# Tail of the first graph layer with sigmoids and masks a step ahead, and the loops of the attention and message layers written out

## The reference

```python
# L0: gated sum over edges, then a GRU and a batch norm
att = sigmoid(x[src] @ W_att[:d] + x[dst] @ W_att[d:] + b_att)
aggregated = segment_sum((x[src] @ W_msg + b_msg) * att, dst)
# L1, three times: attention over the incoming edges
logits = sum(q[dst] * k[src], -1) / sqrt(d)
alpha = softmax of logits within each dst
agg = segment_sum(alpha[:, None] * v[src], dst)
# L3: an MLP of edge features gives weights, multiplied with x[src]
tpw = silu(silu(edge_feats @ A1 + b1) @ A2 + b2) @ A3
message = segment_sum(mji(tpw, x[src], edge_attrs), dst) / 10
```

## Time and profile before

| | |
|---|---|
| median of 3 runs | 7610.16 us (7602.88 to 7610.16) |
| the profiled execution | 7606.87 us, its span 7605.1 us |
| PE, DVE, ACT, POOL busy | 73%, 63%, 28%, 67% of the span |
| attention layers, first to last gather | 1607 to 2674, 2775 to 3832, 3934 to 4989 us |
| message layer, first to last gather | 6449 to 7537 us |
| tail of the first layer | about 1130 to 1463 us |

### The profile page before, as it was taken

The page is one execution under the profiler, slowest core; times in us unless marked ns, Lnnn a source line. Parts: engine busy times, 40 slices in busy tenths (PEclk is TensorE's granted clock), DMA queues, the critical chain, the costliest instruction groups (busy, mean ns, idle before and its releaser), DMA issues. The chain is left out here.

```text
span 7605.1 us, 137273 instructions
## 1 busy us (share of the span) xinstructions
PE 5586.2 (73%) x30113; PEld 4217.7 (55%) x30114; DVE 4809.0 (63%) x20423; ACT 2121.2 (28%) x5508; POOL 5100.1 (67%) x5173
## 2 busy tenths in 40 slices
PE   5664454667767777776777766769899897898887
PEld 4432223345656655666655556656566654676665
DVE  7974433555666655666754766674454545888887
ACT  1033332131111141111141111143343332555554
POOL 5788772447777747777747777737657474777774
PEclk6687777877888787888887888889999998989988
DMA  9422232146677746777746767756667574222222
GB/s 308 122 68 63 71 76 53 36 126 197 205 207 205 205 148 194 208 206 205 209 152 188 210 206 206 206 151 207 176 198 211 161 216 120 55 55 55 55 54 52
DMA packets 911521, 1149.47 MB, mean 151 GB/s; under 512 B 143137, under 2 KB 676193, under 8 KB 911009
## 3 DMA queue, kind: packets, MB, share of 16 engines
q1 hardware_dynamic: 689200, 673.54, 29.4%
q0 software_dynamic: 202464, 461.07, 22.6%
q10 hardware_dynamic: 19346, 9.66, 0.5%
HBM read 882.09 MB, written 261.74 MB: 150 GB/s over the span
## 5 line engine op out<-in xcount | busy, mean ns | idle before, releaser
L486 POOL DMA_INDIRECT G<-table_kv,idx x2496 | 2377.4, 952 | 959.1 <-issue 762.3
L1554 DVE SCALAR_TENSOR_TENSOR sums<-ramp,place,bank 128x128 f32<-128x128 f32 x2496 | 721.9, 343 | 1001.1 <-PE bank L1501 813.5
L1939 POOL DMA_INDIRECT G<-table_h,src_idx x864 | 824.6, 954 | 485.4 <-issue 256.3
L1473 ACT COPY slab<-bank 128x512 f32<-128x512 f32 x624 | 364.9, 585 | 2485.0 <-PE bank L1492 2480.4
L1492 PE MATMUL bank<-ident,G 128*128 128x128 f32 x2496 | 627.7, 338 | 570.9 <-DMA G<-table_kv,idx 565.2
L1501 PE MATMUL bank<-qT,slab 128*128 x4992 | 916.2, 341 | 166.1 <-issue 144.4
L486 POOL DMA_INDIRECT G<-table_h,idx x832 | 835.4, 1004 | 299.3 <-issue 231.3
L534 PE MATMUL bank<-OH,sums 128*128 128x128 f32 x4992 | 858.7, 327 | 143.4 <-DVE sums L523 122.1
L1501 PEld LDWEIGHTS bank<-qT,slab 128*128 128x128 f32 x4992 | 810.6, 246 | 258.4 <-issue 257.9
L514 DVE TENSOR_SCALAR OH<-ramp,place,weight 128x128 f32<-128x128 f32 x2262 | 805.2, 359 | 151.2 <-issue 81.2
L534 PEld LDWEIGHTS bank<-OH,sums 128*128 128x128 f32 x4992 | 763.7, 234 | 195.0 <-issue 73.0
(11 more groups left out here) (342 smaller groups left out, 8868.2 us busy)
## 6 DMA issues: line engine op xcount, KB each, us to landing
stash<-G SPq DMA_DIRECT2D x312, 512.0 KB
sums<-stash SPq DMA_DIRECT2D x624, 256.0 KB
sums<-adjacency SPq DMA_DIRECT2D x294, 522.5 KB
adjacency<-same SPq DMA_DIRECT2D x49, 1184.0 KB
same<-adjacency SPq DMA_DIRECT2D x90, 522.5 KB
G<-table_kv,idx POOLq DMA_INDIRECT x2496
sums<-adjacency SPq DMA_DIRECT2D x48, 408.0 KB
table_kv<-G SPq DMA_DIRECT2D x72, 256.0 KB, 3.1
```

The lines of the kernel that those rows point to most:

```text
L486: pool.indirect_dma_start(G[:, s, 0:width], None, tab, bass.IndirectOffsetOnAxis(ap=idx[:, s:s + 1], axis=0)).then_inc(c_gather[s].sem, 16)
L1473: act.copy(quad(KT, q).rearrange("p s d -> p (s d)"), bank[q % 2][:, :]).then_inc(c_kt.sem, 1)
L1554: ins = dve.scalar_tensor_tensor(scratch[:, s % QUAD, :], ramp[:], place[:, bass.ds(t * SLOTS + s, 1)], bank[2 + q % 2][:, (s % QUAD) * P: ...
L1939: pool.indirect_dma_start(G[:, s, 0:D], None, table[l], bass.IndirectOffsetOnAxis(ap=src_idx[:, DENSE + t:DENSE + t + 1], axis=0)).then_in ...
```

## The change

It has two parts. In the tail of the first layer, ACT's `gates` of a step's quad now stand behind the sigmoids of the next step's mask, and DVE issues the mask (or the placement) of step n + 1 before the adds of step n; `mask(TAIL)` is issued ahead of the loop, and the two first `gate_inputs` ahead of the second mask. SP's, POOL's and PE's lists in the tail stay as they are. In the attention and message layers, the loops over pieces and turns on PE, ACT, DVE (and SP in the message layer) become Python loops: their code is emitted once for each round, with constants in place of registers. POOL's `gather_loop` and SP's loops in the attention layers stay loops.

```diff
-        def turns(engine, body):
-            with engine.Fori(0, TURNS - 1) as i:
-                body(i, False)
-            body(TURNS - 1, True)
+        def turns(body):
+            for i in range(TURNS):
+                body(i, i == TURNS - 1)
...
                     if n == TAIL:
                         gates(FIRST_QUADS)
                         gates(FIRST_QUADS + 1)
-                    if n >= TAIL:
-                        for q in tail_quads(n - TAIL):
+                    if n > TAIL:
+                        for q in tail_quads(n - TAIL - 1):
                             if q + 2 < RUN_QUADS:
                                 gates(q + 2)
+                for q in tail_quads(ALL_STEPS - TAIL - 1):
+                    if q + 2 < RUN_QUADS:
+                        gates(q + 2)
                 act.wait_ge(adj_used.sem, adj_used.at(ALL_STEPS))
...
+                def mask_or_place(n):
+                    if n < ALL_STEPS:
+                        mask(n)
+                    elif n < ALL_STEPS + MASK_CHUNKS:
+                        place_extra(n - ALL_STEPS)
+
+
+                mask_or_place(TAIL)
                 for d in range(TAIL_STEPS):
                     n = TAIL + d
-                    if n < ALL_STEPS:
-                        mask(n)
-                    else:
-                        place_extra(n - ALL_STEPS)
+                    if d == 0:
+                        gate_inputs(FIRST_QUADS)
+                        gate_inputs(FIRST_QUADS + 1)
+                    mask_or_place(n + 1)
                     if n < ALL_STEPS and chunk_before(n) is not None:
                         add_chunk(chunk_before(n))
                     if n > ALL_STEPS:
                         add_chunk(MASK_CHUNKS + n - ALL_STEPS - 1)
                     if d == 0:
-                        gate_inputs(FIRST_QUADS)
-                        gate_inputs(FIRST_QUADS + 1)
                         onehots_and_adds(FIRST_QUADS, None)
...
-        def pieces(engine, body):
-            body(0)
-            body(1)
-            with engine.Fori(0, PIECES - 2) as i:
-                body(i + 2)
-            body(PIECES)
-            body(PIECES + 1)
+        def pieces(body):
+            for c in range(PIECES + 2):
+                body(c)
...
-                with dve.Fori(0, TURNS - 2) as i:
-                    turn(i + 1, False, False)
+                for i in range(1, TURNS - 1):
+                    turn(i, False, False)
```

More of the change, by code:

```diff
@@ L1484, in piece @@
                             act_late_onehots((t - LAG) * QUADS + q + 2)
-            pieces(act, piece)
+            pieces(piece)
         def pe_attention(skip_terms):
@@ L1543, in piece @@
                             pe_sums(t - LAG, q, quad_loaded, v_rows, (4, 5), LATE)
-            pieces(pe, piece)
+            pieces(piece)
         def dve_attention():
@@ L1694, in piece @@
                             take(to)
-            pieces(dve, piece)
+            pieces(piece)
         def act_add_relu(outT):
@@ L2323, in turn @@
                             features(h, (i * 2 + (h + 2)) * PAIR)
-                turns(sp, turn)
+                turns(turn)
             @block.scalar
@@ L2370, in turn @@
                         onehot(i, 5)
-                turns(act, turn)
+                turns(turn)
             @block.tensor
@@ L2426, in turn @@
                         product3(i, 5)
-                turns(pe, turn)
+                turns(turn)
             @block.vector
```

## The result

The changed kernel took **7424.2 us** (median of 4 runs, 7420.3 to 7430.5) beside 7607.6 us (7602.9 to 7610.2) for the kernel before: ratio 0.9763, 95% interval 0.9748 to 0.9777, some 180 us. The forecast was 7439 us. The profiled execution took 7430.5 us with a span of 7428.7.

What follows compares the result with a forecast made beforehand. POOL's gathers bound the attention and message layers, a ring of engines waiting on each other the first layer's tail. 7606.9 - 140 (tail) - 28 (attention) + 0 (message layer) = 7439 us, range 7404 to 7478.

Steps and rivals of the forecast that it cites:

- The sum: Whole kernel: profiled 7606.9 us, less 140 for the tail and 28 for attention, message layer 0, gives 7439 us.
- Long steps: First layer's tail, steps with 418 columns: 7.25 us each after the edit, against 13.65 before.
- the ring: First layer's tail: PE, DVE and ACT wait on each other in turn, 13.65 us; afterwards DVE, ACT, DVE, 7.25 us.
- Short steps: First layer's tail, steps with 272 columns: 6.8 us each after the edit, against 12.8 before.
- Placement steps: Tail's last nine steps, where DVE writes the placement: PE nearly alone, 5.2 us each against 10.1 before.
- The floor of 5.0 from POOL: Placement steps: at PE's faster clock (4.8 us), POOL's 5.0 us of gathers would be the floor.
- The turn of the extra rows: Tail: taken as unchanged at 10.5 us, with ACT's copies still waiting for the same gates and the same product.
- Attention: Three attention layers written out: 28 us gained, four fifths of POOL's 35.5 us lost through DVE's stops at each round.
- rival (a): Only the tail gains, since the softmax burst causes POOL's loss at the attention loop's borders: 7467 us, chance 0.10.
- Message layer: Message layer written out: 0 gained, since nobody holds POOL up; range -25 to +25 us.
- (b): Tail gains less: POOL and DVE block each other at every mask, 9.5 us a step, 7519 us, chance 0.06.
- (c): Slower than before: streaming written-out code stalls engines in attention and message layers, 7654 us, chance 0.03.

## Why the prediction was right, point by point

**The sum** held: 7439 forecast, 7424.2 measured, inside 7404 to 7478. Of the 183 us between the medians (168 forecast by them) the tail has 151 where 140 were forecast, and attention 17 where 28 were. That these two misses cancel is luck; the mechanisms of both were right. The message layer's 7 is not the change's, as the run with that layer alone showed.

**Long steps**, 7.25 forecast, 7.16 to 7.28 measured. The reading of the ring, what leaves it and what stands in its place, is right to a tenth, and the sigmoid that was added on ACT shows that it is this ring. One premise was misread: the 5.57 us of PE's product in the earlier trace rows were taken for the slow clock and are about half at each level. Ten passes at 0.70 us are 7.0, and with the sums that is more than 7.25: at the lower level all through PE would not have been hidden. It never came to that, since the clock rose from 0.76 to 0.91.

**Short steps**, 6.8 forecast; six of them, 1211.31 to 1250.82 us, take 6.6 each. PE's products alternate between 3.0 us, all at the upper level, and some 4.7, partly at the lower (a step whose sums follow after 4.8 to 5.0 us, then one after 8.2 to 8.6), while DVE's masks stay 6.5 us apart.

**Placement steps**, 5.2 forecast, 4.48 measured (40.4 us for nine): the term that was most too large. The floor of 5.0 from POOL isn't a floor over nine steps. POOL fills its 16 slots during the turn before and then stands still:

```profile
1268.32 0.94 POOL L848 DMA_INDIRECT G<-table_gated,src_idx  x1 [5.59 <-PE bank L975]
```

so the quads there start with a store of four. PE at the upper clock, 3.7 + 1.05 less the overlap, sets 4.4 to 4.7. It is 6 us on the sum. Here too the 6.3 us "at the slow clock" was a mixture of the levels; the forecast rested on the clock's rise, which came.

**The turn of the extra rows**, taken as unchanged at 10.5, takes 13.4. What was overlooked: the placement is moved ahead there too, so DVE makes it (1.82 us) before the adds, the gate inputs behind those come later, ACT's last gates wait for them, and the copies for the extra rows stand behind these gates on ACT.

```profile
1257.25 0.15 DVE L1062 TENSOR_TENSOR per_slot<-dst_part,G 128x4 f32<-128x4 f32 x1
...
1257.43 0.20 ACT L913 ACTIVATE per_slot<-per_slot 128x4 f32<-128x4 f32 x1 [3.43 <-DVE per_slot L1062]
1257.55 0.66 ACT L951 COPY sums<-bank 128x272 f32<-128x272 f32 x2
```

That is only a third of it. The copies start 4.0 us after the turn's sums instead of 3.1. The rest, 2.0 us, is PE, which had the lower level nearly all the time (window as above, all engines):

```profile
1257.00:1266.00 9.00, 6.90 (x13) 3.79 (x14) 2.41 (x9) 1.52 (x5) 4.51 (x5) 0.50 0.21 46
```

Its five transposes take 1.33 us instead of 0.77, and the product 6.73 instead of 5.31. The kernel with the placements in their own step agrees: its product starts 5.9 us after the sums instead of 6.9. With the copies first it starts after 3.7, so the order on ACT is on this turn's path; the other 0.8 of the 4.0 us gained there is again a shorter product. The start of the tail came 2.3 us later, not 0.6. Together that is 4.6 us too little, against 6 us too much in the placement, another 6 in the other steps (2 in the long, 2 in the short, 2 in the two irregular ones), and 4 us kept for latencies that didn't show.

**Attention**: the mechanism was right, and the runs that split it leave no room for rival (a). The size: of the 35.5 us of lost pauses 27.2 went, forecast 28. The stage gained only 17.3, because two other things moved. In turn 1 of each layer, outside the loop, one pause grew, put to the store of the stash: 3.17, 4.05 and 3.41 us where it was 0.97, 2.76 and 0.98, so 5.9 us over the layers. And the 2496 gathers got 4.2 us longer in all. A layer's gathers take 1052 to 1057 us, not the 1045 given as a sign. Over ten kernels the three layers sum to 3178.0, 3181.6, 3184.0 and 3193.2 us with DVE's loop, and to 3156.6 to 3169.0, mean 3161.2, in the six without: 23 us between the means. The pause in turn 1 is no steady cost of the written-out code: it is 1.0 to 1.6 us where DVE's code alone is written out and 2.5 to 3.8 with all loops written out, but 2.3 to 2.8 in the kernel with the tail alone, which keeps its loops, and 1.1 to 2.7 in the changed kernel on the third chip. Why, no run tells.

**Message layer**: 0 forecast, 0 measured when it was changed alone.

**Rivals (b) and (c)**: the gather under a mask took up to 3.09 us, dearer than the 2.66 of the earlier trace rows, so it costs 2.1 us and not 1.7. With one in each step POOL would need 5.0 + 2.1 = 7.1 us of 7.2, closer than the forecast thought. It didn't decide, but only just. In the step shown above the gather that met the mask's end took 1.43 us, and POOL had first waited 1.99 us for a free slot; in the two steps after it POOL paused 0.43 or 0.44 us instead of 0.30 before such a gather, 0.13 us from being full. The masks stayed 7.2 to 7.3 us apart in both. Of (c) there is no trace: stops of DVE put to nothing got fewer, and POOL's pauses too.

## What to carry over

When a step is a ring through three engines, write the ring down, cross out what the edit takes out, and compare the next longest ring; then check with an added cost on each engine which one is in it. Count what else the moved operation passes on its queue in the one irregular turn as well as in the regular ones: here that turn was 3 us longer than thought, a third of it by such an order, and putting the copies first more than made up for it. A product's time "at the slow clock" has to be read pass by pass: a wait before it can leave it half at each level, and its mean is then no bound. A floor from an issue rate holds for a long run of steps only; over a few, what lies ready in the buffers counts instead.

## What the runs showed of the hardware

**In the attention loop a branch back on DVE costs 3.75 us, in the message layer's loop nothing.** Over 30 branches the gap behind DVE's branch is 2.9 to 5.0 us in the first, and over 49 at most 0.01 us in the second. The stops go with DVE's attention loop and stay when the others' are removed. The loops differ in length: the trace has 659 records of DVE in a round of the first, 133 in a round of the second. A round of ACT's attention loop has 92 and doesn't stop; one of PE's has 891, in which an f32 matmul leaves several, and doesn't stop either. No run varied the length of a loop alone. A jump out of the window of the prefetch that has to fetch first, as the Trainium skill has it (Runtime: NRT & Kernel Launch, Instruction fetch mechanics), agrees with these rows of DVE; that a fetch fills the gap is not in the trace, and why PE's long loop goes on at once no run shows.

**A mask on DVE delays a gather on POOL, and not the reverse.** A gather of 0.94 us that starts just behind a mask of 2090 columns takes 2.98 to 3.09 us; the mask keeps its 2.34.

**A slower chip.** On one chip, in one group of runs, all kernels took 30 to 31% longer, and the change gained 346 us instead of some 180. There, an operation lasts as long as elsewhere: the page of the changed kernel on it has

```profile
L486 POOL DMA_INDIRECT G<-table_kv,idx x2496 | 2378.5, 953 | 2268.3 <-DMA stash<-G 1050.7 <-issue 871.9 <-ACT idx L472 205.6
```

with the gather's 953 ns beside 954 and the pauses 2268.3 us instead of 938.8. One place where it shows without a DMA to wait for is the weight loads of one line of the first layer: in the changed kernel on that chip (420 to 1150 us) and on the usual one (0 to 460 us) they

```profile
PEld bank L984 <- issue: 577.5, 96, 21.7
```

```profile
PEld bank L984 <- issue: 73.1, 95, 2.2
```

stand still about as often, but 6.0 us each time instead of 0.8, with nothing in the trace to wait for. What it is was not tested, and the larger gain wasn't split into its parts there.
